# Experts stage of a decoder kernel: down's products and y's evictions at other slots, the scatter behind another sum

## Chip, cores and metric

The kernel runs as one program on one core of one Trainium2 chip. The metric is the device time in microseconds of one execution. The median of three runs of the kernel before is 2708.68 us (2708.18 to 2710.73).

## What is computed

A two-layer post-norm decoder on x of 8 x 256 x 512. Only the mixture of experts of the first layer (`_L0_ffn_ref`) is touched by the change. For each of the 2048 tokens it takes the four best of 16 experts, and one shared expert besides:

```python
probs = jax.nn.softmax(x @ gate_w.T, axis=-1)
vals, idx = jax.lax.top_k(probs, K)
w = vals / jnp.sum(vals, axis=-1, keepdims=True)
act = swiglu(jnp.einsum('th,ehi->eti', x, w_gu))     # E=16, H=512, 2I=768
y_e = jnp.einsum('eti,eih->eth', act, w_d)           # silu(gate) * up, then down
out = jnp.einsum('te,eth->th', combine, y_e)
out = out + act_s @ dequant_fp4(shared_down_packed, shared_down_scales)
```

The weights are 4-bit codes with a scale for each group of 128 inputs: gate and up have four groups (512 inputs), down has three (384).

## The kernel before

The stage is `experts`, and every engine runs its own program in it; semaphores tie them together. The work is cut into N = 55 tiles of 256 token slots: tiles 0 to 7 hold the tokens in their own order for the shared expert, tiles 8 to 54 hold tokens sorted by expert. Each tile has six slots (`NO`), o = 0 to 5, and `every_slot` walks over the slots of all tiles and two tiles more, in which only late work is left. Three pairs of slots (gate, then up) make the three blocks n = 3j, 3j+1, 3j+2 of 128 hidden features of tile j.

Path of one block, by line:
- PE, `group` (1295): 8 products of 128x256 into `x_group`, one for each group of inputs and for the high and low part of x. A group waits for the evictions of the group two slots before (two PSUM buffers).
- ACT (1348) evicts the first two quarters of `x_group` with their scales into `x_part`, DVE (1406) adds the last two, each behind ACT's.
- POOL (1261) adds the two halves of `x_part` when gate and up are both there: one sum a block, three a tile.
- ACT takes silu (1354) at slot 2n+3, DVE multiplies gate and up (`product`, 1414) at slot 2n+4, ACT rounds h to its high part (`high`, 1361) at 2n+5, DVE takes the rest (`low`, 1419) at 2n+6. `part` has four buffers, `h` two.
- PE, `down` (1312): y is two halves of 128 tokens by three blocks, six items a tile, each of three fp32r products of 128x512. An item runs behind the group of its slot. Items of half 0 wait for the low part of their block (`h_ready`).
- y's half 0 is evicted by ACT (`out`, 1370), half 1 by DVE (`out`, 1427), in tiles from 8 on with each token's share of the expert. `y` has two buffers.
- Tiles 0 to 7 store y by SP (1210); later ones add it to the tokens' rows in DRAM by two indirect DMAs that POOL issues (`scatter`, 1252). A scatter waits for the landing of the one before (`wait_out`), and for both halves of y.

Besides: the tile after next but one gets its rows by two indirect DMAs of POOL (`gather`, 1240, tile j+3, behind the first sum of tile j); PE turns the rows of tile j+1 (1279) behind slots 1 and 3; ACT copies the high part (`x_high`, 1338) at o=1 and DVE the low part (1398) at o=3; DVE picks each token's share (1441, 1442) at o=5. SP loads the weights of tile j+2 in program order: gate's and up's codes and scales (1180, 1184) when the groups of tile j-1 are done, then down's (1192, two transfers of 768 KB) and `choose` (1197), when y of tile j-1 is done (`y_done`, 1190). Three buffers (`W_RING`).

On each engine the order is the program's: ACT does group, out, high, silu, x_high; DVE does group, out, low, product, x_low, shares; POOL does sum, then gather or scatter. An instruction that waits holds up all behind it.

Of the kernel before, what the change touches and what calls it, by code (L numbers as in the profile page):

```python
# [33 lines left out]
G_D, G_I = D // GS, I_MOE // GS  # L34
# [7 lines left out]
N_SHARED = T // SLOT_TILE  # L42
# [1039 lines left out]
def experts(nc, g, a):  # L1082


    N, M = N_TILES, SLOT_TILE
    NO = 2 * G_I
    PARTS, W_RING, ROWS = 4, 3, 4
    with ExitStack() as ctx:
        def sb(name, shape, dt=F32):
            return ctx.enter_context(nc.sbuf_tensor(f"x_{name}", shape, dt))  # L1090
# [41 lines left out]
        def every_slot(at):  # L1132


            for s in range(NO * (N + 2)):
                at(s // NO, s % NO)
# [7 lines left out]
        def loads(j):  # L1144


            routed = range(N_SHARED, j + 1)
            return 1 + sum(i % W_RING == j % W_RING for i in routed)

        def wait_rows(eng, j):  # L1150
            u = j % ROWS
            if j < N_SHARED:
                eng.wait_ge(own_landed[u], 16 * (j // ROWS + 1))
            else:
                eng.wait_ge(row_landed[u], 16 * HALVES * ((j - N_SHARED) // ROWS + 1))

        def wait_out(eng, j):


            u = j % 2  # L1160
            if j < N_SHARED:
                eng.wait_ge(y_stored[u], 16 * (j // 2 + 1))
            else:
                eng.wait_ge(y_mixed[u], 16 * HALVES * ((j - N_SHARED) // 2 + 1))
# [66 lines left out]
        @block.gpsimd  # L1231
        def _(pool):
            def gather(j):
                u = j % ROWS
                pool.wait_ge(turned, 2 * (j - ROWS + 1))
                if j >= N_SHARED + ROWS:
                    pool.wait_ge(share_ready, j - N_SHARED - ROWS + 1)
                for k in range(HALVES):
                    at = HALVES * (j - N_SHARED) + k
                    pool.indirect_dma_start(out=row[u][:, k, :], out_offset=None, in_=g.rows_dram,  # L1240
                                            in_offset=bass.IndirectOffsetOnAxis(ap=g.rows[:, at:at + 1], axis=0))\
                        .then_inc(row_landed[u], 16)

            def scatter(j):
                u = j % 2
                wait_out(pool, j - 1)
                if j == N_SHARED:
                    wait_out(pool, j - 2)
                for k in range(HALVES):
                    at = HALVES * (j - N_SHARED) + k  # L1250
                    pool.wait_ge((y0_out, y1_out)[k], j + 1)
                    pool.indirect_dma_start(out=g.sum_dram[k], out_offset=bass.IndirectOffsetOnAxis(ap=g.rows[:, at:at + 1], axis=0),  # L1252
                                            in_=y[u][:, k, :], in_offset=None, compute_op=ALU.add)\
                        .then_inc(y_mixed[u], 16)

            for j in range(N + 2):
                for n in range(G_I * j, G_I * (j + 1)):
                    if j < N:
                        x = part[n % PARTS]
                        pool.wait_ge(ev_dve, 4 * (n + 1))  # L1260
                        pool.tensor_tensor(x[:, 0, :, :], x[:, 0, :, :], x[:, 1, :, :], ALU.add).then_inc(summed, 1)  # L1261
                    if n % G_I == 0 and N_SHARED <= j + 3 < N:
                        gather(j + 3)
                    if n % G_I == 1 and N_SHARED <= j - 2:
                        scatter(j - 2)
            for j in (N - 2, N - 1):
                wait_out(pool, j)

        @block.tensor
        def _(pe):  # L1270
            def turn(j, k):
                u = j % ROWS
                if k == 0:
                    wait_rows(pe, j)
                if j >= 1:
                    pe.wait_ge((x_hi_done, x_lo_done)[k], j)
                for half in range(HALVES):
                    for c in range(C):
                        mm = pe.transpose(turn_ps[k][:, c, half * P:(half + 1) * P],
                                          row[u][:, half, 0:D].bitcast(F16)[:, k * D + c * P:k * D + (c + 1) * P], ident[:, :])  # L1280
                mm.then_inc(turned, 1)

            def group(j, o):
                s, u, v = NO * j + o, j % 2, j % W_RING
                if o == 0:
                    pe.wait_ge(gu_landed[v], 32 * loads(j))
                    pe.wait_ge(x_hi_done, j + 1)
                    pe.wait_ge(x_lo_done, j + 1)
                col = (o % 2) * I_MOE + (o // 2) * P
                codes = gu[v][:, :].bitcast(F8).rearrange("p (q n) -> p q n", q=G_D)  # L1290
                for q in range(G_D):
                    if s >= 2 and q % 2 == 0:
                        pe.wait_ge((ev_act, ev_dve)[q // 2], 2 * (s - 1))
                    for k in range(2):
                        mm = pe.matmul(group_ps[s % 2][:, q, :], codes[:, q, col:col + P], xt[u][:, k, q, :],  # L1295
                                       start=k == 0, stop=k == 1)
                    if q % 2:
                        mm.then_inc(group_done, 1)

            def down(j, item):  # L1300
                u, v = j % 2, j % W_RING
                half, k = ((0, 0), (0, 1), (1, 0), (0, 2), (1, 1), (1, 2))[item]
                if item == 0:
                    pe.wait_ge(d_landed[v], 48 * loads(j))
                if half == 0:
                    pe.wait_ge(h_ready, G_I * j + k + 1)

                if k == 0 and j >= 1:
                    pe.wait_ge((y0_out, y1_out)[half], j)
                rows = slice(half * P, (half + 1) * P)  # L1310
                for i, (x, w) in enumerate(((h_hi, d_hi), (h_lo, d_hi), (h_hi, d_lo))):
                    mm = pe.matmul(y_ps[half][:, :], x[u][:, k, rows], w[v][:, k, :],  # L1312
                                   start=k == 0 and i == 0, stop=k == G_I - 1 and i == 2)
                if k == G_I - 1:
                    mm.then_inc(y_done, 1)

            def at(j, o):
                if j < N:
                    group(j, o)
                item = NO * (j - 1) + o - 2  # L1320
                if 0 <= item < NO * N:
                    down(item // NO, item % NO)
                if j + 1 < N and o in (1, 3):
                    turn(j + 1, o // 2)

            pe.wait_ge(ident_ready, 1)
            turn(0, 0)
            turn(0, 1)
            every_slot(at)

        @block.scalar
        def _(act):
# [30 lines left out]
            def out(j):  # L1363
                u = j % 2
                act.wait_ge(y_done, HALVES * j + 1)
                if j >= 2:
                    wait_out(act, j - 2)
                if j >= N_SHARED:
                    act.wait_ge(share_ready, j - N_SHARED + 1)
                act.activation(y[u][:, 0, :], y_ps[0][:, :], ACT.Copy,  # L1370
                               scale=FP8_GAIN * X_GAIN if j < N_SHARED else share[u][:, 0:1]).then_inc(y0_out, 1)

            def at(j, o):
                if j < N:
                    group(j, o)
                if o == 0 and 2 <= j < N + 2:
                    out(j - 2)
                n = lagged(j, o, 5)
                if n is not None:
                    high(n)  # L1380
                n = lagged(j, o, 3)
                if n is not None:
                    silu(n)
                if o == 1 and j + 1 < N:
                    x_high(j + 1)
# [6 lines left out]
        def _(dve):  # L1392
# [51 lines left out]
            def at(j, o):  # L1444
                if j < N:
                    group(j, o)
                if o == 2 and 2 <= j < N + 2:
                    out(j - 2)
                n = lagged(j, o, 6)
                if n is not None:  # L1450
                    low(n)
                n = lagged(j, o, 4)
                if n is not None:
                    product(n)
                if o == 3 and j + 1 < N:
                    x_low(j + 1)
                if o == 5 and N_SHARED <= j < N:
                    shares(j)
# [1267 lines left out]
```

## Time and profile before

| what | us |
| --- | --- |
| median of three runs | 2708.68 |
| the profiled run | 2711.14 |
| its span | 2709.3 |
| experts: first group of PE to last DVE eviction of y | 722.3 to 1394.0 |
| PE busy over the span | 2043.6 (75%) |
| DVE, ACT, POOL busy over the span | 1814.1, 1326.7, 953.4 |

One execution was recorded. The stage of the change takes a quarter of the span. In every view, times are microseconds from the start of the span, unless marked ns; PE is TensorE, DVE VectorE, ACT ScalarE, POOL GpSimd, SP SyncE; L1419 is line 1419 of the kernel. "Idle before <-releaser" is how long the engine stood before an instruction, and what ended that. PEclk is the granted clock of TensorE as a share of full speed, and the DMA share is the mean busy share of the core's 16 DMA engines.

### The profile page before, as it was taken

What the parts mean: (1) busy time and instruction counts of PE and PEld (TensorE: products, weight loads), DVE (VectorE), ACT (ScalarE), POOL (GpSimd) and SP (SyncE); (2) the same over time, 40 slices, a digit from 0 to 9 for tenths busy, and PEclk for the clock granted to TensorE, in tenths of its full rate; (3) what the DMA queues carried; (4) which work ended last, traced back from release to release, by engine and by line L of the source; (5) the groups of instructions that cost most, each with busy time, mean ns of one, the idle gap of its engine ahead of it and who ended that gap; (6) DMA issues with size and microseconds to landing.
All of it is one profiled execution on the core that took longest, in us unless ns stands there. A gap on an engine that the chain in (4) does not pass through costs nothing. (4 is left out here: it accounts for less than half of the span.)

```text
span 2709.3 us, 33393 instructions
## 1 busy us (share of the span) xinstructions
PE 2043.6 (75%) x12168; PEld 1270.0 (47%) x12203; DVE 1814.1 (67%) x2409; ACT 1326.7 (49%) x2139; POOL 953.4 (35%) x547
## 2 busy tenths in 40 slices
PE   2788765126498898988956899997994776789986
PEld 1456642012366666666633566663552332344442
DVE  4349883875776777777744356654443897999975
ACT  0013232655376776766734223323553885556656
POOL 1014443213245777777735122224111000443330
PEclk7888887668699999999987999998997998899998
DMA  3224655001637999999964000002334530000001
GB/s 141 62 93 159 241 189 221 0 0 44 235 102 246 254 251 262 247 261 256 251 152 169 0 1 1 1 1 109 92 80 140 187 118 1 0 1 1 1 0 62
DMA packets 123684, 313.63 MB, mean 116 GB/s; under 512 B 29569, under 2 KB 49537, under 8 KB 119810
## 3 DMA queue, kind: packets, MB, share of 16 engines
q1 hardware_dynamic: 102466, 260.69, 27.8%
q0 software_dynamic: 21056, 50.84, 9.5%
q8 instruction: 96, 1.57, 0.2%
q14 instruction: 66, 0.54, 0.1%
HBM read 219.59 MB, written 92.68 MB: 115 GB/s over the span
## 5 line engine op out<-in xcount | busy, mean ns | idle before, releaser
L1406 DVE SCALAR_TENSOR_TENSOR x_part<-x_group,x_scale,x_part 128x256 f32<-128x256 f32 x660 | 287.9, 477 | 144.2 <-ACT x_part L1348 137.5
L1295 PE MATMUL x_group<-x_xt,x_gu 128*128 128x256 f16 x2640 | 346.2, 275 | 2.1 <-ACT x_part L1348 1.2
L1348 ACT ACTIVATE x_part<-x_group,x_scale 128x256 f32<-128x256 f32 x660 | 276.1, 471 | 123.5 <-PE x_group L1295 117.5
L1261 POOL TENSOR_TENSOR x_part<-x_part 128x512 f32<-128x512 f32 x165 | 235.4, 1431 | 196.7 <-DVE x_part L1406 196.7
L1295 PEld LDWEIGHTS x_group<-x_xt,x_gu 128*128 128x128 fp8e4 x2640 | 237.0, 98 | 85.9 <-issue 32.4
L1312 PE MATMUL x_y_ps<-x_d_hi,x_h_hi 128*128 128x512 f32 x330 | 160.0, 485 | 68.8 <-DVE x_h_lo L1419 66.8
L2418 POOL TENSOR_TENSOR f_part<-f_part 128x1024 f32<-128x1024 f32 x44 | 120.4, 2737 | 188.0 <-DVE f_part L2445 188.0
L154 PE MATMUL mean_n<-residual,const_tables 128*128 128x512 f32 x160 | 79.3, 648 | 138.6 <-PEq L733 103.5
L1754 POOL TENSOR_TENSOR c_pt<-c_pt,const_tables 128x1024 f32<-128x1024 f32 x32 | 75.8, 2369 | 258.4 <-ACT c_pt L1728 258.4
L2316 PE MATMUL f_group<-f_x_hi,f_raw 128*128 128x512 f16 x352 | 138.9, 394 | 32.1 <-DVE f_part L2445 24.6
L1252 POOL DMA_INDIRECT mixed_rows<-x_y,moe_rows x94 | 150.1, 1597 | 31.0 <-issue 20.8
L2182 ACT ACTIVATE z_pt<-z_s 128x1024 f32<-128x1024 f32 x128 | 119.7, 1052 | 51.5 <-PE z_s L2153 50.4
L2445 DVE SCALAR_TENSOR_TENSOR f_part<-f_group,f_scale,f_part 128x512 f32<-128x512 f32 x176 | 123.9, 742 | 26.8 <-ACT f_part L2367 21.1
L2316 PE MATMUL f_group<-f_x_lo,f_raw 128*128 128x512 f16 x352 | 138.0, 392 | 0.0
L2367 ACT ACTIVATE f_part<-f_group,f_scale 128x512 f32<-128x512 f32 x176 | 111.0, 679 | 44.2 <-PE f_group L2316 44.0
L1312 PE MATMUL x_y_ps<-x_d_lo,x_h_hi 128*128 128x512 f32 x330 | 131.1, 397 | 0.0
L1312 PE MATMUL x_y_ps<-x_d_hi,x_h_lo 128*128 128x512 f32 x330 | 130.2, 395 | 0.0
L154 PEld LDWEIGHTS mean_n<-residual,const_tables 128*128 128x128 f32 x160 | 32.9, 209 | 181.6 <-issue 181.6
L1240 POOL DMA_INDIRECT x_row<-token_rows,moe_rows x94 | 102.5, 1091 | 21.5 <-issue 16.4
L1312 PEld LDWEIGHTS x_y_ps<-x_d_hi,x_h_hi 128*128 128x128 f32 x330 | 62.5, 189 | 98.0 <-DVE x_h_lo L1419 92.8
L199 ACT ACTIVATE squares_n<-centred_n 128x2048 f32<-128x2048 f32 x24 | 45.9, 1911 | 127.5 <-DVE centred_n L177 127.5
L2330 PE MATMUL f_y<-f_h_hi,f_w_hi 128*128 128x512 f32 x176 | 104.9, 596 | 3.2 <-DVE f_h_lo L2457 2.2
(331 smaller groups left out, 5042.3 us busy)
## 6 DMA issues: line engine op xcount, KB each, us to landing
x_d_hi<-down_hi SPq DMA_DIRECT2D x50, 768.0 KB, 5.7
x_d_lo<-down_lo SPq DMA_DIRECT2D x50, 768.0 KB, 5.9
x_gu<-codes_gu SPq DMA_DIRECT2D x50, 384.0 KB, 5.7
p_w<-d_s SPq DMA_DIRECT2D x17, 768.0 KB, 7.7
down_hi<-p_hi SPq DMA_DIRECT2D x17, 768.0 KB, 3.9
down_lo<-p_lo SPq DMA_DIRECT2D x17, 768.0 KB, 6.3
aux<-ct SPq DMA_DIRECT2D x2, 4096.0 KB, 16.3
cross_values<-y_v_out SPq DMA_DIRECT2D x16, 512.0 KB, 3.0
```

Source lines behind the costliest of these rows:

```text
L154: mm = pe.matmul(mean_ps[t % 2][:, :], g.const("mean"), tile(src, t)[:, c, :], start=c == 0, stop=c == C - 1)
L1252: pool.indirect_dma_start(out=g.sum_dram[k], out_offset=bass.IndirectOffsetOnAxis(ap=g.rows[:, at:at + 1], axis=0), in_=y[u][:, k, :], in_ ...
L1261: pool.tensor_tensor(x[:, 0, :, :], x[:, 0, :, :], x[:, 1, :, :], ALU.add).then_inc(summed, 1)
L1295: mm = pe.matmul(group_ps[s % 2][:, q, :], codes[:, q, col:col + P], xt[u][:, k, q, :], start=k == 0, stop=k == 1)
L1312: mm = pe.matmul(y_ps[half][:, :], x[u][:, k, rows], w[v][:, k, :], start=k == 0 and i == 0, stop=k == G_I - 1 and i == 2)
L1348: act.activation(part[n % PARTS][:, q, o % 2, :], group_ps[s % 2][:, q, :], ACT.Copy, scale=scale[v][:, o, q:q + 1]).then_inc(ev_act, 1)
L1406: dve.scalar_tensor_tensor(x, group_ps[s % 2][:, 2 + q, :], scale[v][:, o, 2 + q:3 + q], x, ALU.mult, ALU.add).then_inc(ev_dve, 1)
L2182: act.activation(pt[n % RING_P][:, :, :, :], s_ps[n % 3][:, :, :, :], ACT.Exp, scale=HDX ** -0.5)\
L2316: mm = pe.matmul(group_ps[c][:, :], codes[:, n, C * k + c, :], x[t % 2][:, c, :], start=i == 0, stop=i == 1)
L2367: act.activation(part[N % PARTS][:, c, k, :], group_ps[c][:, :], ACT.Copy, scale=scale[:, N % G_F, k, c:c + 1]).then_inc(ev_act, 1)
L2418: pool.tensor_tensor(x[:, 0, :, :], x[:, 0, :, :], x[:, 1, :, :], ALU.add).then_inc(summed, 1)
L2445: dve.scalar_tensor_tensor(x, group_ps[c][:, :], scale[:, N % G_F, k, c:c + 1], x, ALU.mult, ALU.add)\
```

## The change

Three things move; nothing is added or taken away. `DOWN_LAG` is 4 where the code had 2: each item of down runs two slots later, so that item 0 of tile j runs behind the group of slot 4 of tile j+1 and item 5 behind that of slot 3 of tile j+2. The two evictions of y move by two slots: ACT's from o=0 to o=2, DVE's from o=2 to o=4, of tile j+2. On POOL the scatter of tile j-2 stands behind the last sum of tile j, no longer behind the second.

```diff
--- before.py
+++ after.py
@@ -1085,6 +1085,7 @@
     N, M = N_TILES, SLOT_TILE
     NO = 2 * G_I
     PARTS, W_RING, ROWS = 4, 3, 4
+    DOWN_LAG = 4
     with ExitStack() as ctx:
         def sb(name, shape, dt=F32):
             return ctx.enter_context(nc.sbuf_tensor(f"x_{name}", shape, dt))
@@ -1261,7 +1262,7 @@
                         pool.tensor_tensor(x[:, 0, :, :], x[:, 0, :, :], x[:, 1, :, :], ALU.add).then_inc(summed, 1)
                     if n % G_I == 0 and N_SHARED <= j + 3 < N:
                         gather(j + 3)
-                    if n % G_I == 1 and N_SHARED <= j - 2:
+                    if n % G_I == 2 and N_SHARED <= j - 2:
                         scatter(j - 2)
             for j in (N - 2, N - 1):
                 wait_out(pool, j)
@@ -1317,7 +1318,7 @@
             def at(j, o):
                 if j < N:
                     group(j, o)
-                item = NO * (j - 1) + o - 2
+                item = NO * (j - 1) + o - DOWN_LAG
                 if 0 <= item < NO * N:
                     down(item // NO, item % NO)
                 if j + 1 < N and o in (1, 3):
@@ -1373,7 +1374,7 @@
             def at(j, o):
                 if j < N:
                     group(j, o)
-                if o == 0 and 2 <= j < N + 2:
+                if o == DOWN_LAG - 2 and 2 <= j < N + 2:
                     out(j - 2)
                 n = lagged(j, o, 5)
                 if n is not None:
@@ -1444,7 +1445,7 @@
             def at(j, o):
                 if j < N:
                     group(j, o)
-                if o == 2 and 2 <= j < N + 2:
+                if o == DOWN_LAG and 2 <= j < N + 2:
                     out(j - 2)
                 n = lagged(j, o, 6)
                 if n is not None:
```

## Rows read from the trace of the kernel before

**Rows 1.** Windows: busy time of each engine, its instructions, PEclk, DMA share, GB/s.

```profile
735.35:841.74 106.39, 96.44 (x730) 71.22 (x730) 75.67 (x184) 75.34 (x181) 44.24 (x38) 1.00 0.45 153
841.74:870.66 28.92, 23.87 (x166) 17.60 (x165) 17.51 (x44) 16.93 (x41) 17.95 (x15) 0.88 0.81 232
870.66:1366.11 495.45, 445.77 (x3366) 329.46 (x3365) 378.76 (x902) 347.71 (x820) 378.37 (x285) 1.00 0.93 254
```

**Rows 2.** Waits, 745 to 840 us: engine line <- for whom: us, times, longest.

```profile
PE x_y_ps L1312 <- DVE x_h_lo L1419: 8.2, 9, 1.5
```

**Rows 3.** Timeline, one tile: start us, us, engine, line, operation [idle before <-releaser].

```profile
1109.51 1.84 POOL L1261 TENSOR_TENSOR x_part<-x_part 128x512 f32<-128x512 f32 x1
...
1110.69 0.96 DVE L1419 TENSOR_TENSOR x_h_lo<-x_h,x_h_hi 128x256 fp32r<-128x256 f32 x1
...
1111.57 0.41 DVE L1414 TENSOR_TENSOR x_h<-x_part 128x256 f32<-128x256 f32 x1
...
1111.76 0.62 PE L1279 MATMUL x_turn<-x_ident,x_row 128*128 128x128 f16 x8
...
1112.22 1.04 PE L1295 MATMUL x_group<-x_xt,x_gu 128*128 128x256 f16 x8
1112.34 0.40 ACT L1354 ACTIVATE x_part<-x_part 128x256 f32<-128x256 f32 x1
...
1112.64 1.00 ACT L1338 ACTIVATE x_xt<-x_turn 128x1024 f16<-128x1024 f16 x1
1112.85 1.28 POOL L1261 TENSOR_TENSOR x_part<-x_part 128x512 f32<-128x512 f32 x1 [1.49 <-DVE x_part L1406]
...
1113.55 1.73 ACT L1348 ACTIVATE x_part<-x_group,x_scale 128x256 f32<-128x256 f32 x4
...
1113.78 1.05 PE L1295 MATMUL x_group<-x_xt,x_gu 128*128 128x256 f16 x8
1114.12 0.88 DVE L1406 SCALAR_TENSOR_TENSOR x_part<-x_group,x_scale,x_part 128x256 f32<-128x256 f32 x2 [1.35 <-ACT x_part L1348]
...
1114.91 0.74 DVE L1427 TENSOR_SCALAR x_y<-x_y_ps,x_share 128x512 f32<-128x512 f32 x1
1115.57 0.41 DVE L1419 TENSOR_TENSOR x_h_lo<-x_h,x_h_hi 128x256 fp32r<-128x256 f32 x1
1115.60 1.24 POOL L1240 DMA_INDIRECT x_row<-token_rows,moe_rows  x1 [0.30 <-issue]
1115.90 0.42 DVE L1414 TENSOR_TENSOR x_h<-x_part 128x256 f32<-128x256 f32 x1
...
1116.04 0.50 PE L1312 MATMUL x_y_ps<-x_d_hi,x_h_hi 128*128 128x512 f32 x1 [1.20 <-DVE x_h_lo L1419]
...
1116.24 0.87 DVE L1406 SCALAR_TENSOR_TENSOR x_part<-x_group,x_scale,x_part 128x256 f32<-128x256 f32 x2
...
1117.19 1.27 POOL L1261 TENSOR_TENSOR x_part<-x_part 128x512 f32<-128x512 f32 x1 [0.35 <-DVE x_part L1406]
...
1118.61 1.63 POOL L1252 DMA_INDIRECT mixed_rows<-x_y,moe_rows  x1 [0.15 <-issue]
...
1120.54 1.56 POOL L1252 DMA_INDIRECT mixed_rows<-x_y,moe_rows  x1 [0.30 <-issue]
...
1121.59 1.83 POOL L1261 TENSOR_TENSOR x_part<-x_part 128x512 f32<-128x512 f32 x1
```

**Rows 4.** Line 1419, all of it: count, then ns min/median/max, first and last start.

```profile
L1419 DVE TENSOR_TENSOR x_h_lo<-x_h,x_h_hi x165: 408/415/2781, 733.9 to 1390.3; 128x256 fp32r<-128x256 f32 x165
```

**Rows 5.** Timeline of POOL, first scatter of the stage.

```profile
851.52 1.62 POOL L1252 DMA_INDIRECT mixed_rows<-x_y,moe_rows  x1 [3.95 <-DMA mixed_rows<-x_y]
```

**Rows 6.** Timeline, the end of the stage (POOL and DVE).

```profile
1385.01 1.56 POOL L1252 DMA_INDIRECT mixed_rows<-x_y,moe_rows  x1 [0.30 <-issue]
...
1385.38 2.78 DVE L1419 TENSOR_TENSOR x_h_lo<-x_h,x_h_hi 128x256 fp32r<-128x256 f32 x1
...
1390.28 1.56 POOL L1252 DMA_INDIRECT mixed_rows<-x_y,moe_rows  x1 [2.41 <-DMA mixed_rows<-x_y,moe_rows]
```

## Prediction: how the tile's period changes

> **What bounds the kernel now.** I read the windows of the stage first, then one tile of its timeline, engine by engine. The experts stage is the only one touched. The windows [rows 1] run from one x_high (line 1338) to another: those of tiles 1, 10, 12 and 53. Nine early tiles without a scatter take 106.39 us, 11.82 each; 41 later ones take 495.45 us, 12.08 each. PE is busy for 0.90 of either, so it is near its own limit, which is what makes its waits look like the thing to remove. They are waits of down's products for h's low part: 8.2 us in 9 waits in the early tiles [rows 2], 1.20 us in one place of a later tile, at 1116.04 [rows 3].
>
> But in the later tiles POOL and DVE hold the period. Call the sums (line 1261) of a tile sum0, sum1, sum2, the halves of h low (1419) and product (1414), and the slots o=0 to 5. In one later tile [rows 3] sum2 stands in the queue at 1109.51 and ends at 1111.35. The low of o=0, asked for at 1110.69, takes 0.96 instead of 0.41 and ends 0.30 behind the sum; product and DVE's eviction follow, and sum0 starts at 1112.85, 1.50 behind sum2's end. Sum0 and two gathers take 3.99 (1112.85 to 1115.60+1.24). Sum1 waits 0.35 for DVE's eviction, which comes down ACT's x_high 1112.64, eviction 1113.55, DVE's eviction 1114.12, y's eviction 1114.91, low 1115.57. Sum1 and two scatters take 4.91 (1117.19 to 1122.10), and sum2 runs 1.32 behind them, to 1123.42. So 1.50 + 3.99 + 0.35 + 4.91 + 1.32 = 12.07: the whole period, with no step of PE in it. Without the 0.35 it is 11.72.
>
> What makes a low long: its median is 0.415 us, its longest 2.781 [rows 4]. That one (1385.38) began inside a scatter with a sum queued behind it, and lasted until that sum was over [rows 6]. So I let a low that meets a sum, or a scatter with a ready sum behind it, end 0.30 behind the sum.  The Trainium skill, "SBUF — State Buffer", section "Who interferes with whom", says that a VectorE instruction with two SBUF inputs and a GpSimd instruction that reads SBUF exclude each other, whole instruction by whole instruction, the first one winning. The trace agrees on the first half (0.96 for 0.41); a sum held up by a low is in no row. This rule speaks against the change, because it puts a scatter ahead of sum0, whose sum then falls on a low that ran free before.
>
> **The change, part by part.** No instruction is added or removed; the DMAs are the same ones.
>
> 1. Down's products two slots later. Low for o=2 was wanted by the product one slot on; now there are three slots between. PE's 1.2 us wait goes, and the next waits (groups for the evictions two groups back) decide. PE's own floor: group to group 1.56 (1112.22 to 1113.78), a turn 0.46 (1111.76 to 1112.22), so 6 x 1.56 + 2 x 0.46 = 10.3.
> Early tiles: no scatter, POOL has time, sums start as their evictions end and miss the lows. ACT and DVE alone need, by the steps of rows 3, product to silu 0.77, silu to x_high 0.30, to ACT's eviction 0.91, to DVE's 0.57, to low 0.79, to product 0.33, once with x_high (3.7), once without and with y's eviction 0.66 (3.4), once with neither (2.8): 9.9. So PE sets 10.4 (0.1 for x_high, which must wait for the turn). 9 x (11.82 - 10.4) = **-12.8 us**. Bounds: 0 if something else holds them, -13.7 at 10.3.
>
> 2. y's evictions two slots later. DVE's leaves the way from x_high to sum1 and enters that to sum2: 0.66 moved. ACT's comes behind its eviction of o=2, where it delays only that of o=3, which has over 1 us to spare. Weights of down (SP waits for the products) start two slots, some 3.5 us, later, and gate and up's behind them; they are used two periods on, over 20 us, and need about 12: covered. Cover gone, each tile would wait for its codes.
>
> 3. The scatter behind sum2. Walk a later tile from s=0, the start of sum0. Low of o=2 falls on sum0: it ends 1.28+0.30=1.58, product starts 1.50, silu 2.27, ACT's eviction of o=4 2.57, DVE's 3.23 (behind x_low), y's 4.02, low of o=4 4.68. Sum1, behind the gathers, starts at 3.99 and ends at 5.29, so this low is held too, to 5.59. Product 5.51, eviction 5.85, sum2 6.80. Its scatters end at 6.80+4.91=11.71, and sum0 starts. Meanwhile: silu 6.28, evictions 6.58 and 7.15, low of o=0 7.94, held by sum2 to 8.38; product 8.30, silu 9.07, x_high 9.37, evictions 10.28 and 10.85, low of o=2 11.64: inside a scatter with a sum queued, held as in rows 6. The circle closes at **11.72**, the same four pieces as before (3.99 + 4.91 + 1.32 + 1.50) in another order, without the 0.35. 41 x (12.08 - 11.72) = **-14.8 us**. PE (10.3) and the DMA queues are below that: 0.93 of 12.08 is 11.24 us.
>
> 4. Into the scatters. The first one waits 3.95 us for the last plain store, whose issue stands behind SP's wait for the products [rows 5]; both move by two slots, so the stall stays. The two tiles around it take 28.92; they lose one PE wait or two: **-2** (an estimate; from +2 to -4).
>
> 5. The end. Tiles from 52 on gather nothing, so the circle is 2.6 shorter and falls under PE's floor: two tiles of some 10.8 instead of 11.72, **-2** (0 to -3). The last scatters follow each other, each waiting for the one before to land [rows 6], from the third last on. That one stood 1.42 behind sum1 (1117.19 to 1118.61); it will stand 1.42 behind sum2, which in the walk is 6.80-3.99: **+2.8**. Two of down's products that ran beside groups now run behind the last one, under this chain: 0.
>
> Sum: -12.8 -14.8 -2 -2 +2.8 = -28.8 us. The profiled run took 2711.14 with a span of 2709.3; the median of three is 2708.68. So a span of 2680.5, and a median of **2680**.
>
> **Rivals.** (a) The lock goes the other way. Low of o=2 starts 0.07 before sum0 in my walk. If sum0 has to wait for it (0.34), the period is 12.05, step 3 brings 1.2 us and the time is 2693. For: a first-come rule and a margin of 0.07. Against: rows 6.
>
> (b) The queues bind. 0.93 of the span is DMA; at 11.24 a tile they are full. If lows and sums miss each other more than I say, this ends it: 41 x 0.48 less, 2660.
>
> (c) No new collision, POOL (10.4 of work) and PE beside each other at 10.4 to 10.8: 41 x 1.3 to 0.9 less, 2626 to 2642. For: the steps allow it if low and product of o=2 both pass ahead of a late sum0. Against: that holds silu up as long as the lock would (sum0 ends 0.74+1.28 behind low's start, silu would else go 1.10 behind it: 0.9 a tile). By the rule named above it can't last either, as sum0 and low come 0.1 us apart.
>
> (d) Slower. All three sums, not one as now, meet their low at its start: each costs 1.28+0.30-0.41=1.17, and 9.9 + 3 x 1.17 = 13.4 a tile, 2749. It decides from where step 3 costs what the rest brings: 11.72 + 28.8/41 = 12.42. For: POOL has 10.4 us of work in order, and the scatter, moved ahead of sum0, is late for silu of o=3. Against: sum2 and its low overlap for 0.1 only in the walk.
>
> (e) The PE wait was only a symptom in the early tiles too, and low of o=2 goes the other way: within 0.2%, 2709.
>
> **Chances.** Forecast (11.5 to 11.9 a tile, 2673 to 2688) 0.50; (a) 0.13; (b) 0.13; (c) 0.10; (d) 0.09; (e) 0.05. Low 2655 takes in (b), high 2700 takes in (a) and the bounds of steps 1, 4 and 5. A measurement of this kernel tells 0.2%, 5.4 us, from no change. Faster 0.86, same 0.05, slower 0.09.
>
> **What would show it.** Waits of PE for `x_h_lo` near zero: step 1. Early tiles at 10.4: step 1. Later tiles at 11.7, three long lows in each, those of o=2 and o=4 by over 0.5 us: step 3; lows of 0.41 with shorter tiles: (c). POOL without idle time but for the 1.50 ahead of sum2: the circle. Last scatter later behind sum1 of the last tile by 2.8: step 5. DMA share at 1.0: (b). A sum queued behind a low would make (a) right, and the forecast wrong.

## The result, and the profile after

The changed kernel takes 2676.16 us in the median of its runs (2668.52 to 2676.86), before it was 2708.68; the ratio is 0.987, 95% interval 0.9841 to 0.9898. Its profiled run took 2676.86 with a span of 2675.1, which is 34.2 less than the 2709.3 of before. Of the four executions of run 4 below, one took 8104.59 us at a mean granted clock of 0.255; it counts in that run's median, but not in its ratio. These are the same three windows as [rows 1], again from the x_high of tile 1 to those of tiles 10, 12 and 53 (its line is 1339 now; every line of the stage is one further down).

```profile
736.68:829.87 93.19, 92.45 (x729) 71.11 (x730) 73.61 (x184) 73.28 (x180) 44.40 (x37) 1.00 0.49 160
829.87:855.47 25.60, 21.78 (x166) 15.84 (x165) 18.55 (x45) 16.27 (x41) 15.96 (x13) 1.00 0.86 270
855.47:1326.90 471.43, 445.82 (x3364) 322.64 (x3363) 409.85 (x903) 328.89 (x821) 369.48 (x286) 1.00 0.93 267
```

An early tile takes 93.19 / 9 = 10.35 (before 11.82), a later one 471.43 / 41 = 11.50 (before 12.08). PE's busy time in the later tiles is what it was (445.82, before 445.77); in the early ones it is 92.45 for 96.44, with the same products. DVE's busy time rises by 31 us over the later tiles, with the same instructions. The timeline of POOL and DVE in one later tile says where that is; the column in brackets is the idle time before an instruction and who ended it.

```profile
1060.00 1.29 POOL L1262 TENSOR_TENSOR x_part<-x_part 128x512 f32<-128x512 f32 x1 [1.49 <-DVE x_part L1407]
1061.44 1.62 POOL L1253 DMA_INDIRECT mixed_rows<-x_y,moe_rows  x1 [0.16 <-issue]
1063.38 1.57 POOL L1253 DMA_INDIRECT mixed_rows<-x_y,moe_rows  x1 [0.30 <-issue]
1064.41 1.83 POOL L1262 TENSOR_TENSOR x_part<-x_part 128x512 f32<-128x512 f32 x1
1066.41 1.02 POOL L1241 DMA_INDIRECT x_row<-token_rows,moe_rows  x1 [0.16 <-issue]
1067.73 0.97 POOL L1241 DMA_INDIRECT x_row<-token_rows,moe_rows  x1 [0.31 <-issue]
1068.72 1.28 POOL L1262 TENSOR_TENSOR x_part<-x_part 128x512 f32<-128x512 f32 x1
1071.49 1.29 POOL L1262 TENSOR_TENSOR x_part<-x_part 128x512 f32<-128x512 f32 x1 [1.49 <-DVE x_part L1407]
...
1061.15 0.42 DVE L1420 TENSOR_TENSOR x_h_lo<-x_h,x_h_hi 128x256 fp32r<-128x256 f32 x1
...
1064.83 1.71 DVE L1420 TENSOR_TENSOR x_h_lo<-x_h,x_h_hi 128x256 fp32r<-128x256 f32 x1
...
1069.62 0.66 DVE L1420 TENSOR_TENSOR x_h_lo<-x_h,x_h_hi 128x256 fp32r<-128x256 f32 x1
1070.21 0.41 DVE L1415 TENSOR_TENSOR x_h<-x_part 128x256 f32<-128x256 f32 x1
1070.55 0.86 DVE L1407 SCALAR_TENSOR_TENSOR x_part<-x_group,x_scale,x_part 128x256 f32<-128x256 f32 x2
```

The sums are, from the top, sum2, sum0, sum1 and the next sum2. The record of a sum that is queued behind a DMA issue starts early (1064.41): it really starts where the second scatter ends, at 1064.95. Follow POOL round: sum2 and its scatters 4.95 (1060.00 to 1064.95), sum0 and the gathers 3.77 (to 1068.72), sum1 1.28 (to 1070.00). Then POOL idles for 1.49, because the low of o=4 (1069.62) was held until sum1 was over, and DVE's eviction for sum2 stands behind it. 4.95 + 3.77 + 1.28 + 1.49 = 11.49: the whole period again. PE is not in it.

PE's wait for `x_h_lo` [rows 2, 3] is gone: in before it came to 8.2 us in the early tiles and 49.7 us, in 42 waits, in the later ones, and after has none. What PE still waits for between 900 and 1300 us is DVE's eviction of the groups, 0.3 at the most (line, whom it waits for: us, times, longest):

```profile
PE x_group L1296 <- DVE x_part L1407: 14.0, 45, 0.3
```

All lows together, as in [rows 4]:

```profile
L1420 DVE TENSOR_TENSOR x_h_lo<-x_h,x_h_hi x165: 407/666/2549, 735.3 to 1350.3; 128x256 fp32r<-128x256 f32 x165
```

The median low is now a held one, 0.666 for 0.415: two of three in each later tile.

The balance of the span: start of the stage +1.3, early tiles -13.2, the two tiles around the first scatter 28.92 to 25.60 = -3.3, later tiles -24.0. From tile 53's x_high to the next stage's first instruction it is 48.4 where it was 44.1, +4.3. That is -34.9; +0.7 lies elsewhere.

### The profile page after: what moved, and what is told of

Its sections match the earlier page's. It is cut to its first block and busy times, and to the rows that moved or that the text cites. A ratio compares the mean times of both kernels' runs of the same rounds, so it can differ in the third digit from the quotient of the medians.

```text
span 2675.1 us, 33393 instructions
## 1 busy us (share of the span) xinstructions
PE 2039.2 (76%) x12168; PEld 1262.2 (47%) x12203; DVE 1845.3 (69%) x2409; ACT 1304.8 (49%) x2139; POOL 945.1 (35%) x547
## 5 line engine op out<-in xcount | busy, mean ns | idle before, releaser
L1296 PE MATMUL x_group<-x_xt,x_gu 128*128 128x256 f16 x2640 | 362.0, 275 | 33.5 <-DVE x_part L1407 20.3
L1296 PEld LDWEIGHTS x_group<-x_xt,x_gu 128*128 128x128 fp8e4 x2640 | 229.5, 98 | 140.7 <-issue 61.5
L1349 ACT ACTIVATE x_part<-x_group,x_scale 128x256 f32<-128x256 f32 x660 | 264.2, 472 | 11.7 <-PE x_group L1296 11.4
L1362 ACT ACTIVATE x_h_hi<-x_h 128x256 fp32r<-128x256 f32 x165 | 68.8, 417 | 168.0 <-DVE x_h L1415 141.8
L1420 DVE TENSOR_TENSOR x_h_lo<-x_h,x_h_hi 128x256 fp32r<-128x256 f32 x165 | 137.5, 833 | 0.5 <-ACT x_h_hi L1362 0.5
L177 DVE TENSOR_TENSOR centred_n<-residual,mean_n 128x2048 f32<-128x2048 f32 x20 | 45.7, 2286 | 89.6 <-PE mean_n L154 89.6
```

The costliest lines, as they stand in the source:

```text
L1349: act.activation(part[n % PARTS][:, q, o % 2, :], group_ps[s % 2][:, q, :], ACT.Copy, scale=scale[v][:, o, q:q + 1]).then_inc(ev_act, 1)
L1420: dve.tensor_tensor(h_lo[j % 2][:, n % G_I, :], h[n % 2][:, :], h_hi[j % 2][:, n % G_I, :].bitcast(F32), ALU.subtract).then_inc(h_ready, 1)
```

## Experiments

Two theories went in. **Lock**: the tile is a circle of POOL and DVE, in which lows are held by sums (the forecast). **PE wait**: what counts is PE's wait for the low, and where the scatter stands is of no account. Diffs are against the kernel after, unless marked otherwise, and show the main lines; "..." marks what is left out. "Early" and "later" are us a tile over the same windows as above.

**1. The lag without the moved scatter.**

```diff
-                    if n % G_I == 2 and N_SHARED <= j - 2:
+                    if n % G_I == 1 and N_SHARED <= j - 2:
```

> The changed kernel with the scatter put back behind the second sum of the tile; down's products and y's evictions stay two slots later. My theory: the steady period is a circle of POOL and DVE (three sums, two gathers, two scatters, and 1.49 us from the end of a sum that held a low up to the next sum), whose length does not depend on where the scatter stands. Then the tiles from 12 to 53 take 11.45 to 11.7 us each, as in the changed kernel (11.50), with one long low a tile instead of two, the nine early tiles 10.35 us, and the time is 2672 to 2682 us. Rival: the scatter had to move, since its second half now waits for y's eviction at slot 4 and holds the last sum up: a POOL wait for x_y in each tile, 12.0 us or more a tile, and 2690 us or more.

Measured: 2672.66 (ratio 0.9871, 0.9855 to 0.9888), early 10.33, later 11.53. This is the window of its later tiles, and its long low:

```profile
855.38:1328.11 472.73, 449.21 (x3367) 319.96 (x3366) 411.00 (x903) 333.81 (x821) 370.51 (x285) 1.00 0.89 266
```

```profile
1106.21 2.02 DVE L1420 TENSOR_TENSOR x_h_lo<-x_h,x_h_hi 128x256 fp32r<-128x256 f32 x1
...
1105.04 1.58 POOL L1253 DMA_INDIRECT mixed_rows<-x_y,moe_rows  x1 [0.30 <-issue]
1106.10 1.84 POOL L1262 TENSOR_TENSOR x_part<-x_part 128x512 f32<-128x512 f32 x1
1109.43 1.28 POOL L1262 TENSOR_TENSOR x_part<-x_part 128x512 f32<-128x512 f32 x1 [1.49 <-DVE x_part L1407]
```

So the lag alone brings all of the gain. The low of o=0 begins inside the second scatter, with sum2 queued, and is over at 1108.23, 0.29 behind the sum (1107.94). The circle is that of before without its 0.35, and with a second gather of 0.97 (at 1112.18) for 1.24: in before, sum1 waited for DVE's eviction, with y's eviction (0.66) in the path to it [rows 3], and in run 1 it starts right behind the gathers (1113.18). That it is the move of y's eviction that took this wait away, and not that of the products, is read from the path; the two were not moved apart.

**2. The scatter without the lag.** Lag 2 as in before, y's evictions at o=0 and o=2, the scatter behind sum2. This diff is against the kernel before.

```diff
-                    if n % G_I == 1 and N_SHARED <= j - 2:
+                    if n % G_I == 2 and N_SHARED <= j - 2:
```

> The kernel before with only the scatter moved behind the last sum; down's products and y's evictions at their old slots. My theory: the circle alone sets the steady tiles, so they take 11.5 to 11.7 us as in the changed kernel, though PE still waits for h's low part (up to 1 us a tile); the nine early tiles, which have no scatter, stay at 11.8 us. Time 2683 to 2692 us. Rival (down's lag is what frees the steady tiles): they stay at 12.0 or more, and the time is 2705 to 2712 us.

Measured: 2698.76 (0.996, 0.9946 to 0.9974), early 11.82, later 11.87. A miss, by 6.8 us beyond the range: I had only POOL's circle in mind. In the later tiles no low is held, and PE waits for the low, once a tile:

```profile
865.15:1351.99 486.84, 445.60 (x3364) 329.30 (x3363) 358.94 (x902) 347.71 (x820) 378.56 (x286) 1.00 0.87 259
```

```profile
1117.19 0.74 DVE L1427 TENSOR_SCALAR x_y<-x_y_ps,x_share 128x512 f32<-128x512 f32 x1
1117.85 0.41 DVE L1419 TENSOR_TENSOR x_h_lo<-x_h,x_h_hi 128x256 fp32r<-128x256 f32 x1
...
1118.32 0.50 PE L1312 MATMUL x_y_ps<-x_d_hi,x_h_hi 128*128 128x512 f32 x1 [0.98 <-DVE x_h_lo L1419]
...
1119.12 0.62 PE L1279 MATMUL x_turn<-x_ident,x_row 128*128 128x128 f16 x8
```

The waits between 900 and 1250 us, as above:

```profile
ACT x_part L1348 <- PE x_group L1295: 66.5, 117, 1.1
PE x_y_ps L1312 <- DVE x_h_lo L1419: 30.0, 30, 1.3
```

Y's eviction and the low stand ahead of down's products, these ahead of the turn (1119.12) and the next groups, and the groups' evictions ahead of the next low: 11.87 a tile, close to an early tile of before (11.82), which had this circle alone. No engine waits for a sum here. So the kernel before had **two circles of nearly one length**, PE's (11.87, as run 2 has it) and POOL's (12.08). The moved scatter opens only the second, and stops at the first. The lag opens the first, and shortens the second from 12.08 to 11.53: the 0.35 of sum1's wait, and most of the rest by the shorter gather.

**3. A sum that reads nothing.** The addition of two parts is left out: a fill writes both, so the gate and up values are wrong and only the time counts.

```diff
-                        pool.tensor_tensor(x[:, 0, :, :], x[:, 0, :, :], x[:, 1, :, :], ALU.add).then_inc(summed, 1)
+                        pool.memset(x[:, :, :, :], 0.5).then_inc(summed, 1)
```

> The changed kernel with the sum of POOL replaced by a fill of the whole block with a constant: the sum of the two halves is left out (and so what follows computes on a constant), POOL reads no SBUF there. If it is the sum's reading of SBUF that holds h's low part up, no low is longer than 0.45 us, and the steady tiles fall from 11.50 to what PE and the rest allow, 10.4 to 10.8 us (2630 to 2648 us in all). If POOL's writes hold DVE up as well, the lows stay long and the tile at 11 us or more. If the DMA queues bind (0.93 busy at 11.50 us: 10.7 us of work a tile), the tile stops at 10.7 to 11.2 with a DMA share near 1.0. The fill may be shorter than the sum's 1.28 us, which by itself would take 0.3 us or so for each sum out of POOL's circle; the duration of the lows tells the cases apart.

```profile
849.98:1278.02 428.04, 427.52 (x3365) 329.65 (x3364) 349.69 (x902) 338.69 (x820) 331.06 (x286) 1.00 1.01 294
```

```profile
L1420 DVE TENSOR_TENSOR x_h_lo<-x_h,x_h_hi x165: 408/415/425, 730.9 to 1297.9; 128x256 fp32r<-128x256 f32 x165
```

No low is held, of 165 (none is over 0.425); a later tile takes 10.44, an early one 10.39, and PE is busy for 427.52 of 428.04. POOL's work is shorter too (331.06 busy for 369.48, 0.94 a tile), about as much as the 1.06 that a tile fell by; so this run alone shows the hold gone, not its price. Its time is 2623.01 in the profiled run and 2652.14 in another, a spread that I can't explain; nothing rests on it.

**4. One half of the scatter behind sum1, the other behind sum2.** POOL does the same work as in after.

```diff
-                    if n % G_I == 2 and N_SHARED <= j - 2:
-                        scatter(j - 2)
+                    if n % G_I >= 1 and N_SHARED <= j - 2:
+                        scatter(j - 2, n % G_I - 1)
...
```

> The changed kernel with the two halves of the scatter apart: half 0 behind the second sum, half 1 behind the last. The same instructions, POOL's work spread more evenly. My theory: the first sum of the next tile then starts 3 us behind the start of the last one instead of 4.95, when its evictions are done, and ends before the low of slot 2; the sum behind the gathers ends before the low of slot 4. At most the low of slot 0 meets a sum. The steady tiles fall to 10.4 to 10.9 us, the time to 2635 to 2655 us. If POOL's total of instructions were the bound and not the collisions, the tile would stay at 11.5 us and the time at 2676; if the DMA queues bind, 11.0 to 11.2 us a tile with a DMA share near 1.0, and 2656 to 2664.

Measured: 2632.83 (0.9715, 0.9696 to 0.9735), later 10.61; the two tiles around the first scatter take 28.22, since that scatter now waits 8.30 for the last plain store. Windows, then POOL and DVE in one tile:

```profile
856.22:1291.42 435.20, 431.36 (x3366) 327.05 (x3365) 352.38 (x902) 335.69 (x820) 369.59 (x285) 1.00 0.99 289
```

```profile
1112.16 1.54 POOL L1263 TENSOR_TENSOR x_part<-x_part 128x512 f32<-128x512 f32 x1
1113.87 1.01 POOL L1241 DMA_INDIRECT x_row<-token_rows,moe_rows  x1 [0.16 <-issue]
...
1116.18 1.29 POOL L1263 TENSOR_TENSOR x_part<-x_part 128x512 f32<-128x512 f32 x1
1117.64 1.62 POOL L1254 DMA_INDIRECT mixed_rows<-x_y,moe_rows  x1 [0.17 <-issue]
1119.84 1.28 POOL L1263 TENSOR_TENSOR x_part<-x_part 128x512 f32<-128x512 f32 x1 [0.58 <-DVE x_part L1408]
...
1114.21 0.41 DVE L1421 TENSOR_TENSOR x_h_lo<-x_h,x_h_hi 128x256 fp32r<-128x256 f32 x1
...
1118.21 0.41 DVE L1421 TENSOR_TENSOR x_h_lo<-x_h,x_h_hi 128x256 fp32r<-128x256 f32 x1
```

This gives the price, down to the next bound. POOL's instructions are those of after (busy 369.59 against 369.48), only 5 of the 123 lows of the later tiles are over 0.45 us (in after 80), and a tile is 0.89 shorter: PE (431.36 of 435.20) is the bound. Most of what is left to PE is a wait for the scales of gate and up, which after doesn't have; between 900 and 1250 us it is:

```profile
PE x_group L1297 <- DMA x_scale<-gu_s: 2.8, 5, 0.8
```

With 3.2 us of issues in one piece POOL falls behind and its sums meet the lows; with 1.6 at a time POOL is early enough to wait for DVE ahead of one sum in most tiles (36 waits in 41 tiles, mostly 0.6), and the lows of o=2 and o=4 begin 0.5 and 0.7 behind a sum's end. The low at 1118.21 lies inside a scatter with no sum queued, and takes 0.41.

**5. The kernel after, once more,** as the measure of runs 6 to 8.

> The changed kernel as it is, for comparison on the same chip as the three below: steady tiles 11.50 us, early tiles 10.35 us, the two tiles around the first scatter 25.6 us, 2668 to 2677 us in all.

Measured: 2673.34 (0.9867, 0.985 to 0.9883), early 10.46, later 11.51.

**6. More work for PE.** The turns of x are done twice, to the same result.

```diff
-                for half in range(HALVES):
+                for half in 2 * list(range(HALVES)):
```

> The changed kernel with the eight transposes of each turn done twice (the same result): 0.46 us more of PE in two slots of each tile, 0.92 us a tile. My theory: PE is in no circle of the steady tiles, so they stay at 11.50 us; the nine early tiles, which PE paces, go from 10.35 to 11.2 or 11.3 us. Time 7 to 11 us more than the changed kernel. Rival: PE, 0.95 busy in the steady tiles, is the bound: they take 12.4 us and the time is 45 us more.

```profile
736.18:836.05 99.87, 99.76 (x869) 78.55 (x867) 74.69 (x184) 74.59 (x180) 44.63 (x38) 1.00 0.45 146
...
862.50:1334.54 472.04, 470.48 (x4020) 362.92 (x4019) 402.39 (x902) 335.84 (x820) 370.24 (x286) 1.00 0.95 267
```

Early 11.10, +0.64 a tile (a little under the 11.2 to 11.3 expected: the second turns keep PE busy for some 0.6 and not 0.92), but later 11.51, +0.01, at a PE busy for 470.48 of 472.04. In all 2681.25 (0.99, 0.9884 to 0.9917). PE sets the early tiles and has 0.6 us free in a later one, as the circle says.

**7. More work for POOL.** A fill of a spare 128x256 tile behind the gathers.

```diff
+        spare = sb("spare", [P, M])
...
                         gather(j + 3)
+                        pool.memset(spare[:, :], 0.0)
```

> The changed kernel with one more instruction of POOL in each tile behind the gathers, a fill of 128x256 that nobody waits for (some 0.3 us of engine time by the fill of that size elsewhere in the profile, 0.4 with what lies around it). My theory: POOL is in the circle with all that it does, so the steady tiles go from 11.50 to 11.8 or 11.95 us, the early ones stay at 10.35 us, and the time is 12 to 19 us more than the changed kernel. Rival: POOL idles 1.5 us a tile, the fill fits in there, and nothing changes.

```profile
855.63:1337.49 481.86, 446.31 (x3371) 323.38 (x3370) 420.24 (x903) 328.91 (x821) 380.74 (x326) 1.00 0.92 261
```

Later 11.75, +0.25, a little under the 11.8 expected; the fill holds POOL for 0.28. In all 2686.34 (0.9917, 0.9901 to 0.9934), +13.0, of which 41 x 0.25 = 10.3 are in the later tiles. What POOL gets to do is paid nearly in full, what PE gets to do, not at all: after is bound by POOL's circle.

**8. The last plain stores ahead of the loads.** SP issues store(j-2) before it waits for the products that free the weights.

```diff
+                if 2 <= j < N_SHARED + 2:
+                    store(j - 2)
                 if N_SHARED <= j + 2 < N:
...
-                if 2 <= j < N_SHARED + 2:
-                    store(j - 2)
```

> The changed kernel with SP's plain store of y (tiles 0 to 7) issued ahead of the loads of the same step instead of behind them. My theory: the first scatter waits for the last store, which stands behind SP's wait for down's products of the next tile; now it lands a tile earlier, POOL's wait of 3.5 us at the first scatter goes, and the two tiles around it take 21 to 22.5 us instead of 25.6. Steady tiles stay at 11.50. Time 3 to 5 us less than the changed kernel. Rival: the gates' codes, now behind the store on SP, come late and PE waits for them in tiles 8 to 10; no gain.

```profile
829.69:851.91 22.22, 21.56 (x167) 15.93 (x166) 18.59 (x45) 16.16 (x42) 15.97 (x13) 1.00 0.85 267
```

The two tiles around the first scatter take 22.22 for 25.60, and that scatter no longer waits. In all 2669.45 (0.985, 0.9834 to 0.9867), 3.9 less than run 5. So the stall was SP's order, in after and, as the code is the same there, in [rows 5].

**9. Runs 4 and 8 together.**

> Both together, on the changed kernel: half 0 of the scatter behind the second sum, half 1 behind the last (as in the run of that edit alone, 2633 us, steady tiles 10.6 us), and SP's store ahead of its loads. The split makes the first scatter want its data a slot earlier, and it waited 8.3 us there; with the store a tile earlier that wait goes, and the two tiles around it take 21 to 22 us instead of 28.2. Time 2625 to 2629 us. If the wait is for something else than the store, 2633.

Measured: 2627.55 (0.9703, 0.9687 to 0.9719), two tiles around the first scatter 21.16, later 10.55.

**10. The halves apart.** In 9 the second half's scatter of a tile also holds the next tile's first half back, by one common semaphore; here each half has its own.

```diff
-            eng.wait_ge(y_mixed[u], 16 * HALVES * ((j - N_SHARED) // 2 + 1))
+            for k in halves:
+                eng.wait_ge(y_mixed[u][k], 16 * ((j - N_SHARED) // 2 + 1))
...
```

> The kernel of the run above, with a semaphore for each half of the scatter: a half waits only for the same half of the tile before, since the two halves go to different tensors. In the steady tiles nothing waits there, so they stay at 10.6 us. At the end of the stage, where each scatter waits for the landing of the one before, the last three tiles' scatters follow each other in about 5.3 us instead of 7.1: 3 to 4 us less, 2622 to 2625 us. If the DMA queue and not the wait paces them there, no gain.

```profile
829.10:850.39 21.29, 21.25 (x166) 16.00 (x165) 17.10 (x45) 16.39 (x42) 17.56 (x14) 1.00 0.88 280
850.39:1283.67 433.28, 429.76 (x3357) 326.53 (x3356) 351.17 (x903) 336.59 (x821) 369.97 (x286) 1.00 0.99 291
```

```profile
1302.41 1.56 POOL L1255 DMA_INDIRECT mixed_rows<-x_y,moe_rows  x1 [0.16 <-issue]
1304.94 1.60 POOL L1255 DMA_INDIRECT mixed_rows<-x_y,moe_rows  x1 [0.97 <-DVE x_y L1430]
1307.21 1.56 POOL L1255 DMA_INDIRECT mixed_rows<-x_y,moe_rows  x1 [0.67 <-DMA mixed_rows<-x_y,moe_rows]
1309.84 1.55 POOL L1255 DMA_INDIRECT mixed_rows<-x_y,moe_rows  x1 [1.07 <-DMA mixed_rows<-x_y,moe_rows]
1312.23 1.56 POOL L1255 DMA_INDIRECT mixed_rows<-x_y,moe_rows  x1 [0.84 <-DMA mixed_rows<-x_y,moe_rows]
```

**2620.84** (0.9676, 0.966 to 0.9692): the fastest here. It is 6.7 less than 9, where I expected 3 to 4, but the two intervals overlap. What the edit does is seen at the end: from tile 53's x_high to the last scatter it is 28.56, in run 9 32.21, so 3.65 less, as expected. The later tiles are as in 9 (10.57); the last scatters now follow each other by 2.3 to 2.6 us, while in after a pair follows a pair by 7. Most later tiles take 10.43 to 10.49, about one in five 10.9 to 11.1. PE waits for the scales of gate and up in six places of runs 4 and 10, 3.5 and 3.2 us in all, so part of this is weights that come late; the rest is open.

## Why the prediction was right, step by step

**Bound of the kernel now.** Half right. POOL's circle with the 0.35 was there (runs 1, 7). What I missed is that PE's wait in the later tiles was not idle beside it: run 2 shows a PE circle of 11.87 right under it. My expectation for that run, which knew of POOL's circle alone, was off by 6.8 us or more.

**Step 1.** Right: 10.35 against 10.4, -13.2 against -12.8; PE's waits for the low are gone, it is busy 92.45 of 93.19, and run 6 confirms that it is the bound there.

**Step 2.** No load or code waited; the cover held. But I told this step as a move of 0.66 from one path to another. It is what pays in the later tiles (run 1).

**Step 3.** The walk was right, one term was not. From the start of sum0 (1064.95), walk against trace: low of o=4 4.68 / 4.67, sum2 6.80 / 6.54, low of o=0 behind sum2's start 1.14 / 1.15, low of o=2 ahead of the next sum0 0.07 / 0.12, and it is held to 1.58 / 1.59. Lows of o=2 and o=4 held: yes. That of o=0 I had held as well, but its own 0.42 ends 0.28 behind the sum anyway, so nothing of it shows. The mis-sized term is sum0 with the gathers, 3.99 taken from [rows 3], 3.77 measured. In before, the second gather (1115.60) started 0.03 behind a low and took 1.24; now it starts with no low near and takes 0.97. So sum1 is 0.22 earlier, its low is held by 0.25 rather than the "over 0.5" I gave, and the period is 11.50 instead of 11.72. That is 41 x 0.22 = 9 us more gain: -24.0 for -14.8.

And the cause I gave for that gain, the scatter's new place, is wrong in the steady tiles: run 1 has 11.53 without it. What the move does is at the edges. Two tiles around the first scatter: 25.6 with it, 29.5 without (run 2 against before, 23.7 to 28.9). After tile 53: 48.4 with it, and 43.5 without (1328.11 to 1371.6). It brings some 4 and costs some 5, which is nothing in sum: 0.987 with it, 0.9871 without, intervals one over the other.

**Step 4.** -3.3 against -2, inside its bounds. The forecast left out the granted clock of this stretch, which is 0.88 of full speed in before and 1.00 in after. What that is worth isn't shown apart; run 5, the kernel after at 0.93 there, takes 25.73, only 0.13 more. The stall moved with the products as I said (3.49 for 3.95 of [rows 5]), and run 8 removes it. The first scatter of after:

```profile
842.82 1.62 POOL L1253 DMA_INDIRECT mixed_rows<-x_y,moe_rows  x1 [3.49 <-DMA mixed_rows<-x_y]
```

**Step 5.** +4.3 against +0.8. I ended the last tiles at PE's 10.8, but two scatters stay. Without the gathers sum1 comes early and its low runs free, yet the low of o=2 is still held behind scatters and sum0. By my own walk sum2 then starts at about 6.3, and 6.3 + 4.91 = 11.2. This is POOL in tile 53 and 54 of after:

```profile
1335.49 1.29 POOL L1262 TENSOR_TENSOR x_part<-x_part 128x512 f32<-128x512 f32 x1 [2.20 <-DVE x_part L1407]
...
1346.58 1.29 POOL L1262 TENSOR_TENSOR x_part<-x_part 128x512 f32<-128x512 f32 x1 [2.13 <-DVE x_part L1407]
...
1354.94 1.55 POOL L1253 DMA_INDIRECT mixed_rows<-x_y,moe_rows  x1 [3.49 <-DMA mixed_rows<-x_y,moe_rows]
...
1361.94 1.55 POOL L1253 DMA_INDIRECT mixed_rows<-x_y,moe_rows  x1 [3.58 <-DMA mixed_rows<-x_y,moe_rows]
```

1346.58 - 1335.49 = 11.09, as that sum says. So the -2 didn't come: from tile 53's x_high to the last sum1 it is 16.26, in before 15.61, +0.65. The first scatter behind that sum1 starts 4.86 later, in before 1.43, so the +2.8 was +3.4. From there to the last scatter it is as before (15.78 and 15.96).

The total, 2676.2 for 2680, owes part of its closeness to two misses of opposite sign: 9 us too little in step 3, some 3.5 too little cost in step 5.

**Rivals.** (a) fell: the low goes ahead of sum0 and is held by it (1.71), 0.12 ahead instead of 0.07. (b) fell as a mechanism: the DMA share is 0.93 at 12.08 and at 11.50 a tile, 0.99 at 10.6 and 1.01 at 10.44 (run 3), so share times period is no floor at 11.2. At 10.6, though, PE begins to wait for weights (runs 4 and 10), so how far below that the queues would let a tile go isn't shown. (c) did not happen here, but runs 4, 9 and 10 are it, at 10.55 to 10.61. (d) fell: two locks a tile, of which only that of o=4 stands in the circle, not three. (e) fell: the early tiles went down to PE's floor.

## What to carry to other kernels

When an engine seems to wait for one thing, walk the whole period and close every circle, as there may be two of nearly one length; an edit that opens one gives only the difference to the next. Before a block of work is moved in an in-order queue, ask whether it can be cut in two: here the move gave nothing, the cut some 40 us. And take a duration out of a trace only with what ran beside it, since the 1.24 of one gather went with its place beside a low, and was gone when the place was.

## What the hardware showed beyond the forecast

A low that begins inside a scatter is not held as such (0.41 at 1118.21 in run 4), but with a sum queued behind the scatter it lasts until the sum is over: 1.71 in after, 2.02 in run 1. All 84 long lows of after end 0.28 to 0.31 behind a sum. The Trainium skill, "SBUF — State Buffer", section "Who interferes with whom", says that a VectorE instruction with two SBUF inputs excludes a GpSimd one that reads SBUF, but not one that only writes it. Run 3 agrees: a fill of 128x1024 in place of each sum, and 165 lows between 408 and 425 ns. That a sum holds the low while it is still queued stands in this case's rows alone (after, run 1 and [rows 6]).

A gather's issue takes 1.22 to 1.27 when it starts less than 0.1 behind the start of a low (36 in before, 37 in run 2, as at 1117.90 behind the low of 1117.85), and 0.94 to 1.04 otherwise, but for one to three a trace between 1.10 and 1.23. That the low is the cause is argued from these places, not tried by itself. A sum held up by a low was again in no row.

Left open: the spread of after's own runs (2668.5 to 2676.9), and a start of the stage that differs by up to 5 us from run to run (tile 1's x_high from 732.1 to 736.7).
